# One program for two attention stages: the causal stage's opening dealt into the last steps of the cross attention

## What is computed

```python
def reference(x, ctx_1024, mask_BxS2_bf0, g_xattn, g_ffn, ...):
    x = x + jnp.tanh(g_xattn[0]) * _L0_xattn_ref(_layernorm(x), ctx_1024, ctx_1024, mask_BxS2_bf0, ...)
    x = x + jnp.tanh(g_ffn[0]) * _L0_ffn_ref(_layernorm(x), ...)
    return x

def _L0_xattn_ref(query, key, value, ...):
    scores = jnp.einsum('bqhd,bkhd->bhqk', Q, K) / math.sqrt(D_K) + bias[None]
    attn = jax.nn.softmax(scores, axis=-1)
    return jnp.einsum('bhqk,bkhd->bqhd', attn, V).reshape(Bsz, S, D_MODEL) @ Wo + bo

def _L0_ffn_ref(x, ...):
    x = x + _attention(_rmsnorm(x, w_ln1), Wq, Wkva, Wkvb, Wo)   # causal, softmax over 16 heads
    residual = x
    return residual + _moe(_rmsnorm(x, w_ln2), Wgate, ...)
```

## Time and profile before

| | us |
|---|---|
| median of 3 runs (lowest, highest) | 2393.33 (2389.95, 2396.13) |
| the profiled execution: its own time | 2390.08 |
| its span, first to last instruction | 2388.2 |
| PE busy in the span | 2129.7 (89%) |
| DVE, ACT, POOL busy | 1505.1, 1178.9, 1364.8 |

### The profile page before, as it was taken

The page is one execution under the profiler, slowest core; times in us unless marked ns, Lnnn a source line. Parts: engine busy times, 40 slices in busy tenths (PEclk is TensorE's granted clock), DMA queues, the critical chain, the costliest instruction groups (busy, mean ns, idle before and its releaser), DMA issues. The chain is left out here.

```text
span 2388.2 us, 43597 instructions
## 1 busy us (share of the span) xinstructions
PE 2129.7 (89%) x12672; PEld 972.8 (41%) x12673; DVE 1505.1 (63%) x4218; ACT 1178.9 (49%) x2316; POOL 1364.8 (57%) x1452
## 2 busy tenths in 40 slices
PE   3899999999999963899999999999985787899997
PEld 1333333333333311344444444444433343455554
DVE  3788888888888843566566566565534577344443
ACT  3355555555555442355545455454445474455554
POOL 3267767677677670265656555655651565455554
PEclk7999999999999986899999999999997898999999
DMA  5413323232232203544534345253403675666665
GB/s 173 151 58 105 101 84 116 70 109 94 89 107 76 84 6 131 146 122 118 150 95 142 117 132 143 88 152 98 142 32 134 125 163 117 109 117 115 111 110 88
DMA packets 222851, 263.78 MB, mean 110 GB/s; under 512 B 39192, under 2 KB 165004, under 8 KB 222388
## 3 DMA queue, kind: packets, MB, share of 16 engines
q1 hardware_dynamic: 197612, 212.79, 29.6%
q0 software_dynamic: 22976, 48.38, 11.7%
q10 hardware_dynamic: 2072, 0.28, 0.1%
HBM read 162.12 MB, written 86.80 MB: 104 GB/s over the span
## 5 line engine op out<-in xcount | busy, mean ns | idle before, releaser
L496 ACT ACTIVATE a_pt<-a_bank 128x512 f32<-128x512 f32 x512 | 305.2, 597 | 361.1 <-DVE a_bank L603 357.7
L1382 DVE CUSTOM_DVE_ANT_0 b_bank<-b_bank,b_tri 128x256 f32<-128x256 f32 (+3 forms) x512 | 253.8, 497 | 303.0 <-PE b_bank L1519 298.2
L614 DVE CUSTOM_DVE_ANT_0 a_bank<-a_bank,a_strip 128x512 f32<-128x512 f32 x512 | 353.4, 691 | 4.9 <-PE a_bank L757 4.0
L1167 POOL TENSOR_TENSOR b_acc<-b_acc,b_pt 128x256 f32<-128x256 f32 (+2 forms) x384 | 271.3, 727 | 89.5 <-ACT b_pt L1256 72.3
L406 POOL TENSOR_TENSOR a_acc<-a_acc,a_pt 128x512 f32<-128x512 f32 x256 | 317.1, 1274 | 3.6 <-ACT a_pt L496 3.1
L603 DVE TENSOR_TENSOR a_bank<-a_bank,a_band 128x256 f32<-128x256 f32 (+1 forms) x512 | 205.9, 403 | 132.2 <-PE a_bank L744 130.9
L1256 ACT ACTIVATE b_pt<-b_bank 128x256 f32<-128x256 f32 (+2 forms) x384 | 144.0, 384 | 190.1 <-PE b_bank L1503 179.6
L744 PE MATMUL a_bank<-a_q_stack,a_k_stack 128*128 128x512 f16 x512 | 196.3, 385 | 12.2 <-ACT a_pt L496 11.8
L757 PE MATMUL a_bank<-a_k_stack,a_q_stack 97*128 97x512 f16 x512 | 196.1, 383 | 3.6 <-DVE a_low L614 3.5
L1849 POOL DMA_INDIRECT out_dram<-c_z,c_to_row x72 | 114.1, 1585 | 138.2 <-DMA out_dram<-c_z,c_to_row 101.2
L403 POOL TENSOR_TENSOR a_acc<-a_pt 128x512 f32<-128x512 f32 x128 | 160.0, 1271 | 4.3 <-ACT a_pt L496 4.3
(11 more groups left out here) (346 smaller groups left out, 5439.4 us busy)
## 6 DMA issues: line engine op xcount, KB each, us to landing
b_q_stack<-qk_rows SPq DMA_DIRECT2D x192, 128.0 KB, 2.7
a_q_stack<-qk_rows SPq DMA_DIRECT2D x96, 128.0 KB
a_k_stack<-qk_rows SPq DMA_DIRECT2D x96, 128.0 KB
b_k_stack<-qk_rows SPq DMA_DIRECT2D x96, 128.0 KB, 2.7
a_sums<-in_x SPq DMA_DIRECT2D x34, 256.0 KB, 2.9
qk_rows<-a_qk_hi SPq DMA_DIRECT2D x64, 128.0 KB, 1.7
qk_rows<-a_qk_lo SPq DMA_DIRECT2D x64, 128.0 KB, 1.8
out_dram<-a_sums SPq DMA_DIRECT2D x32, 256.0 KB, 2.0
```

The costliest lines, as they stand in the source:

```text
L496: nc.scalar.activation(pt[:, n % SLOTS, :], st_bank[n % 2][:], ACT.Exp).then_inc(exped, 1)
L614: nc.vector.tensor_tensor_reduce(out=max_bank[step % 2][:], in0=max_bank[step % 2][:], in1=strip[:, g * HG + hh, at:at + S], scale=-1.0, s ...
L1167: nc.gpsimd.tensor_tensor(sums_of, sums_of, probs(n), ALU.add).then_inc(pooled, 1)
L1382: nc.vector.tensor_tensor_reduce(out=max_bank[step % 2][:, 0:w], in0=max_bank[step % 2][:, 0:w], in1=tri[:, at:at + w], scale=-1.0, scalar ...
```

## The change

The five engine programs of `pass_a` and `pass_b` become Python generators that yield once a step (SyncE's at three places). A new function `run_both` puts them in one block. `pass_a`'s steps are numbered through, 0 to 639; with step 558 (`B * UNITS + JOIN`, step 46 of the body `last`) the first step of `pass_b`, with what stands ahead of its loop, is issued behind it, and so on one for one. So steps 0 to 17 of `pass_b`'s `first` go behind steps 46 to 63 of `last`, and steps 18 to 47 behind steps 0 to 29 of `end`. In front of step 48 (`HANDED`) PE, DVE, ACT and POOL wait for `pass_a`'s last `O`.

```diff
+def run_both(nc, one, two):
+    joined = B * UNITS + JOIN
+    def merged(first, second):
+        for at, _ in enumerate(first):
+            if at >= joined:
+                next(second)
+        for _ in second:
+            pass
+    with nc.Block() as block:
+        @block.sync
+        def _(sp):
+            second = two.sync(sp)
+            for _ in one.sync(sp):
+                next(second)
+            for _ in second:
+                pass
+        @block.gpsimd
+        def _(pool):
+            merged(one.gpsimd(pool), two.gpsimd(pool))
...
```

```diff
-        stage = pt[:].rearrange("p (s k) n -> p s (k n)", s=2)
+        stage = [ht_hi[:].rearrange("p k n -> p (k n)").bitcast(F32), ht_lo[:].rearrange("p k n -> p (k n)").bitcast(F32)
+                 ] + [sums[:].rearrange("p t n -> p (t n)")] * 3
...
-        SPLITS = {0: 11, 1: 13, 2: 15, 3: 17, 4: 36}
+        SPLITS = {0: 0, 1: 1, 2: 2, 3: 9, 4: 50}
...
+        first_place = {(HT, 0): 3, (HT, 1): 4, (HT, 2): 3, (HT, 3): 4, (LAT, 0): 3, (KSW, 0): 4, (QN, 0): 3, (K, 0): 4, (QR, 0): 2,
+                       (QN, 1): 3, (QSW, 0): 4, (K, 1): 2, (QR, 1): 4, (QSW, 1): 2}
+        places = job_bank + max_bank
...
+                    if kind == "first" and step == HANDED:
+                        pe.wait_ge(first_pass.left_dve, first_pass.upto((O, NT - 1)))
...
-            for s in used:
-                pool.sem_clear(s)
-            pool.wait_ge(const_set, 1)
-            over(pool, body)
+            pool.wait_ge(const_set, 1)
+            yield from over(body)
+            for s in first_pass.used:
+                pool.sem_clear(s)
```

More of the change, by code:

```diff
@@ L52 @@
 SHIFT = P.bit_length() - 1
+JOIN = 46
 def unit_of(n):
@@ L1103, in _ @@
             sp.sem_inc(z1_stored, 16)
-            over(sp, body)
+            yield from over(body)
             sp.wait_ge(z1_stored, 64 * B + 16)
@@ L1239, in body @@
                 for step in range(STEPS):
+                    if kind == "first" and step == HANDED:
+                        act.wait_ge(first_pass.left_dve, first_pass.upto((O, NT - 1)))
                     n = step - L
@@ L1400, in _, with tensor @@
             dve.wait_ge(const_loaded, 80)
-            over(dve, body)
-        @block.tensor
-        def _(pe):
+            yield from over(body)
+        def tensor(pe):
             mm = nc.tensor.matmul
             def free(kind, b, job):
-                mine = [j for j in names if j in present[kind] and place[j] == place[job]]
+                mine = [j for j in names if j in present[kind] and place(kind, j) == place(kind, job)]
                 prior = [j for j in mine if pieces[j][0] < pieces[job][0]]
```

257 lines of the change are left out of this document (152 added, 105 removed).

## The result

| | us |
|---|---|
| before, median of 4 runs (lowest, highest) | 2393.69 (2389.95, 2396.13) |
| after, median of 4 runs (lowest, highest) | 2360.12 (2358.49, 2363.00) |
| ratio after to before, 95% interval | 0.9862 (0.9845 to 0.9880) |
| span of the profiled execution, before and after | 2388.2 and 2357.6 |

The change is 33.6 us faster, by the interval 29 to 37. The forecast was 2351.0, range 2336 to 2370: direction and range hold. Of the 9.1 us between forecast and result, 6.0 are gain that didn't come (39.6 forecast) and 3.1 the start of the reckoning: the profiled execution of before lies 3.6 under its median, and the forecast was rounded up by 0.5.

The account below looks back on a forecast made before the run. PE bounds the passes' inner parts; between them each window has another limit. The first bound moves from 977.95 to 937.4, gaining 40.6, less 1.0: 39.6 us off 2390.1 gives 2350.5, forecast 2351, range 2336 to 2370.

Parts of the forecast that it names:

- The empty window: Between the passes, 908.3 to 922.5: only some memsets compute while engines meet and constants load; its 14.2 us go entirely.
- the stretch: From unit 40's exponential in `last` to step 48 of `pass_b`, the first bound on PE: 122.3 us before, 40.6 saved.
- in group 3 POOL stays the bound: Attention's last steps: transposes, scaled input and latent product hide beside 16 us of POOL sums, so group 3 adds nothing.
- POOL's backlog: At step 46, some three POOL sums of 1.23 us still queued behind ACT; 3.7 us taken off the 15.2 of stops.
- Group 2: Its sum over keys on PE comes 11.5 us later through stops, splits and norm, plus 3 us for holding.
- The holding of DVE's splits by POOL: `pass_b`'s thirteen splits at four of `pass_a`'s steps are held by POOL additions sharing SBUF: 3 us in the sum.
- the rival: Splits held by POOL at full size: 16 us in place of 3, on the way to group 2's sum; 2364, chance 0.15.
- Part two: Group 3's sum over keys to step 48: 1.9 us, 17 matmuls at 0.43, 95 at 0.217, 2 for banks, 0.7 rotation; ends 937.4.
- the stacks of group 0 are in time: Before the first bound: SyncE's 13 issues take 7 us and, with two stores between, end some 4 us before PE.
- After step 48: Later stacks of group 1 cost nothing; the output weight's split moving into this window costs 1 us.
- Semaphores: POOL clears them at the end instead of `pass_b`'s start: between nothing and 4.6 us, taken as nothing.
- part one: Step 46 of `last` to step 5 of `end`, up to group 3's sum over keys: 890.4 before, 904.9 forecast.

Follow-up runs that it names:

- e1: The change with the join moved to 94, behind the end body's last instruction: one block and early loads, no overlap; 2379.47 us, ratio 0.9949.
- e2: The change with the join at 64, the start of the end body, the last two weights loaded behind two residual loads; 2359.78 us, ratio 0.9856.
- e8: As e5, but in the opening DVE computes each transposed tile's low part a step later; 2357.45 us, ratio 0.9847.
- e3: The change with DVE's seven memsets and ACT's constants moved behind the splits, off the path at the join; 2359.05 us, ratio 0.9862.
- e7: The change with the edits of e3, e4, e5 and e6 together; 2354.13 us, ratio 0.9833.
- e6: The change with group 0's rotated queries stored and read back by ACT's queue instead of SyncE's; 2358.04 us, ratio 0.9857.
- e9: As e5, with the join at step 55 of the last body and SyncE's order as in e2; 2364.70 us, ratio 0.9878.
- e11: As e9, but SyncE issues group 0's stacks ahead of the cross attention's last two stores; 2361.77 us, ratio 0.9859.
- e5: The change with the next batch's input load issued ahead of the stacks of groups 1 and 2 in the opening; 2353.69 us, ratio 0.9841.
- e4: The change with SyncE issuing the causal stage's loads only after group 2's mask row has landed; 2359.24 us, ratio 0.9854.
- e0: The changed kernel again, unaltered, as the measure of chance; 2361.32 us, ratio 0.9865.

## Why the prediction was right and where it was wrong

**The empty window, 14.2 us: right.** e1 keeps this part of the change and the early loads, with nothing laid beside `pass_a`, and gains 13.5 us in time and 17.0 in the stretch.

**The overlap is most of the gain: right in size, wrong in place.** 22.2 us of stretch beyond e1. But 19.6 of them come from the end body's 23.8 us, as e2 shows (105.3 - 85.7); I had counted on the attention steps being POOL-bound, so that what is put beside them is free. It isn't: "in group 3 POOL stays the bound" is the step that failed. From sum 2 to sum 3 took 21.7 us before and 27.1 after, forecast unchanged. The windows between the two sums, before and after:

```profile
868.73:890.38 21.65, 11.91 (x53) 2.02 (x54) 6.45 (x16) 8.88 (x16) 17.07 (x14) 0.74 0.00 1
885.13:912.26 27.13, 20.48 (x81) 6.83 (x82) 9.79 (x22) 13.27 (x24) 17.36 (x14) 0.70 0.16 56
```

POOL does the same 17 us of work and now stands for 10 of 27; PE is the busiest engine, at a mean clock of 0.70, and no engine is full. POOL's backlog, on which I took 3.7 off and let the whole of group 3 hide, is gone at the first stop. The sum over keys of group 3 came at 54.0 where I had 49.2. Two things can make up the 5.4 us: the hand-overs between engines, of which e8 moves one and gets 0.8, and PE's clock, which is 0.85 in the two traces with the same order where this interval is shortest (25.7 and 25.8 us) and 0.70 to 0.80 in the five where it is 26.3 to 28.0. Their shares stay open; even at 0.85 it is 4 us over before.

- Group 2: forecast 11.5 plus 3 for the holding, measured 26.9 - 13.1 = 13.8. Right within a microsecond, though by other shares: the stops are whole (unit 40's exponential to unit 43's is 14.1 us for three steps and was 3.2, so 10.9 for the 10.6 forecast) and the holding is small.
- The holding of DVE's splits by POOL: forecast 3, rival 16. Thirteen instructions took 1.01 + 1.34 + 3.23 + 2.76 = 8.3 us, before 1.11 + 0.68 + 2.74 + 2.73 = 7.3. My mark for "wrong about the holding" was 2.7 for four: one quartet has 2.76, the other 3.23. It exists, at 1.1 us net, in two instructions: `b_wb_lo` (1.34 for 0.68) and the first of the first query quartet. Each started while a POOL sum ran (865.27 + 1.26 = 866.53 and 868.13 + 1.26 = 869.39) and ended 0.5 us behind that sum's end, so each was held for what was left of it, 0.5 to 0.7 us here and about a whole one in the earlier trace rows. The Trainium skill (GPSIMD Engine Reference, Specifications) states that POOL's SBUF interfaces are shared with VectorE, with contention where a DVE instruction has two SBUF inputs; the traces agree at these two places. It was mostly absent because POOL stood waiting for ACT, as the rival's "against" had it, and e3 and e7 show the other case: with POOL busy, the first four splits took 3.31 us instead of 1.01. So the rival was right about the mechanism and wrong about how often it would meet a busy POOL.

**Part two: forecast 32.5, measured 29.1, for reasons that partly cancel.** PE's clock was granted in full from the first product (0.38 us each, 0.22 apart from 913.3 on; the window has 1.00), so the 17 matmuls at 0.43 didn't happen: 3.6 us less. The sum over keys took 1.0 instead of 1.9, and the 2 us for bank changes and the 0.7 for the last rotation product didn't show (the products run without a gap up to 937.3): 3.5 less. Against that, "the stacks of group 0 are in time" failed: the first bound waits 3.60 us for a DMA, my own mark for being wrong. 32.5 - 3.6 - 3.5 + 3.6 = 29.0. I had counted SyncE's issues for the stacks and not the rotated queries' own round trip, which is last and stands behind a store, a wait and a load of the cross attention. e6 gets 1.7 of the 3.6 back by another queue. The price of an order on this queue shown by itself is in e9 and e11: 7.0 us of stretch for two stores ahead of the stacks or behind them.

**After step 48: forecast 1.0, measured 3.9 to the 49th bound.** "Nothing comes of it" holds for the stacks themselves; what I missed is what SyncE has to issue behind them. The load of the next batch's input was issued 21.1 us after the first bound (962.43 - 941.31) where it was 17.7, and DVE waited 3.41 us for it, with bounds queued behind. Its issue before:

```profile
995.64 0.40 SPq L1069 DMA_DIRECT2D b_xn<-out_dram  x1
```

e5 moves that one load and the loss is 0.6, with the split of the output weight, for which I had put the 1.0, still in it.

**Semaphores, nothing: right** (12.10 against 12.09 us). **Everything else unchanged: not quite.** The early loads (4.0 MB) delay a mask row by 2.6 us; e4 and the other traces show that POOL's sums hide all but 0 to 2.1 us of it. The 1.9 us at the start and 2.8 behind the last bound of `pass_b` belong to no step of mine; e0 and the others say how far they are spread.

**The sum.** Forecast stretch gain 40.6, measured 39.2 (38.4 in e0). That it fits within 1.4 us is in part luck: part one came 4.8 us later than forecast (54.0 for 49.2) and part two was 3.4 shorter. The rest of the 6 us is the 2.9 us after step 48 and what differs outside the change between one execution and the next.

**A version that beats before and very likely the change:** e5, at 2353.7 us (0.9841, interval 0.9825 to 0.9857). Its interval still touches the change's; the traces leave less doubt: from the 481st bound of `pass_a` to the 49th of `pass_b` are 190.2 us against 195.9 and 198.8 in the two traces of the change. The other two kernels joined at 46 with this edit, e7 and e8, have 189.6 and 190.4, the three without it, e3, e4 and e6, 195.9 to 196.9.

## What to carry to other kernels

When two chains are laid into one program order, count on what is put beside a stretch being paid there unless an engine has a measured backlog that lasts through it; the gain comes from laying work beside a stretch in which the engines stand idle, here the output product's chain. Then go through the queue of the engine that issues the DMAs item by item, as its own timeline: which waits in it belong to the other chain, and what is queued behind them. The place of two stores in SyncE's order was worth 7 us of stretch at one join, and that of one load some 4 us over the 48 bounds; 18 further steps of overlap were worth 2 to 4.

## What the runs showed that I had not expected

- PE's granted clock was 1.00 in the 29 us behind two windows of 0.56 and 0.70: from 908.3 on, ahead of sum 3, PE's matmuls in a row were 0.22 us apart, and the products ran at full rate from the first on. With the join at 64, where the 23 us ahead of sum 3 had 0.50, the first eight products ran at the lower level, some 0.43 us apart: three ahead of a gap of 3.5 us and five behind it (e2, 905.2 to 912.6).
- PE waited 2.6 us for a single row of 4 KB that was issued (839.72) while 4.0 MB of loads on another queue were on their way, and not at all when the loads were issued six microseconds later, behind the row (842.08 instead of 835.77).
- Executions of the same code differ by 3.5 us in their first 100 us and by 2.1 from `pass_b`'s last bound to the end, while the 715.0 us between the 25th and the 481st bound agree to 0.12 us in all of them.
